# Self attention core: key blocks four heads wide on both row halves, softmax denominators along rows on VectorE, probabilities divided by GpSimd before they are turned

## The reference

```
s[b, h, i, j] = sum_e q[b, h, i, e] * k[b, h, j, e] * 16 ** -0.5     (j > i masked out)
p[b, h, i, :] = exp(s - max_j s) / sum_j exp(s - max_j s)
a[b, h, i, :] = sum_j p[b, h, i, j] * v[b, h, j, :]
x += a @ Wo
```

## Time and profile before

| | us |
|---|---|
| median of the three runs | 3569.16 |
| lowest and highest run | 3563.95 and 3569.59 |
| the profiled execution's own time | 3562.83 |
| its span | 3561.0 |
| TensorE busy in the span | 3273.7 (92%) |
| VectorE, ScalarE, GpSimd busy | 1697.1 (48%), 1383.5 (39%), 550.4 (15%) |

### The profile page before, as it was taken

How to read it: one execution, slowest core, us unless ns; L and a number is a source line. 1 busy time by engine, 2 the same in 40 slices (tenths; PEclk the granted TensorE clock), 3 DMA queues, 4 the chain that set the end, 5 groups by cost and what they waited for, 6 DMA issues and landing times. The chain is left out here.

```text
span 3561.0 us, 57170 instructions
## 1 busy us (share of the span) xinstructions
PE 3273.7 (92%) x22593; PEld 2122.6 (60%) x22597; DVE 1697.1 (48%) x3600; ACT 1383.5 (39%) x2368; POOL 550.4 (15%) x354
## 2 busy tenths in 40 slices
PE   4899999996999789999999889989999999678898
PEld 3567777774445354577777657654577777434444
DVE  5535555543232255566666234345566665455222
ACT  3335665531111132466666122222466666323221
POOL 4322122100216025300000000005200000203000
PEclk8889999997999889999999999999999999878899
DMA  1032221311211112022211110012122221100011
GB/s 29 26 104 55 61 63 47 62 38 52 88 59 56 40 33 67 20 50 51 51 47 36 45 33 28 23 40 67 28 48 44 49 51 32 32 11 21 27 40 35
DMA packets 184554, 158.98 MB, mean 45 GB/s; under 512 B 77780, under 2 KB 155590, under 8 KB 182352
## 3 DMA queue, kind: packets, MB, share of 16 engines
q1 hardware_dynamic: 184288, 155.32, 16.3%
HBM read 115.16 MB, written 18.09 MB: 37 GB/s over the span
## 5 line engine op out<-in xcount | busy, mean ns | idle before, releaser
L1720 ACT ACTIVATE l1x_shared<-l1x_shared,l1x_a_low 128x1500 f32<-128x1500 f32 x112 | 173.1, 1545 | 189.5 <-DVE l1x_shared L1676 189.5
L1720 ACT ACTIVATE l2x_shared<-l2x_shared,l2x_a_low 128x1500 f32<-128x1500 f32 x112 | 173.1, 1546 | 188.7 <-DVE l2x_shared L1676 186.4
L1720 ACT ACTIVATE l0x_shared<-l0x_shared,l0x_a_low 128x1500 f32<-128x1500 f32 x112 | 173.3, 1547 | 187.1 <-DVE l0x_shared L1676 178.0
L1611 PE MATMUL l0x_a_T_ps<-ident,l0x_shared 128*125 128x128 f32 x1344 | 176.1, 281 | 15.5 <-issue 14.7
L1611 PEld LDWEIGHTS l0x_a_T_ps<-ident,l0x_shared 128*125 128x125 f32 x1344 | 155.2, 187 | 39.6 <-issue 38.0
L1611 PE MATMUL l2x_a_T_ps<-ident,l2x_shared 128*125 128x128 f32 x1344 | 176.5, 281 | 0.8 <-ACT l2x_shared L1720 0.8
L1611 PE MATMUL l1x_a_T_ps<-ident,l1x_shared 128*125 128x128 f32 x1344 | 176.5, 281 | 0.8 <-ACT l1x_shared L1720 0.8
L1595 PE MATMUL l1x_a_S_ps<-l1x_kt,l1x_a_q 64*128 64x375 f32 x896 | 172.0, 501 | 1.4 <-DMA l1x_a_q<-l1x_qa 0.8
L1611 PEld LDWEIGHTS l2x_a_T_ps<-ident,l2x_shared 128*125 128x125 f32 x1344 | 155.2, 187 | 29.8 <-issue 28.2
L1611 PEld LDWEIGHTS l1x_a_T_ps<-ident,l1x_shared 128*125 128x125 f32 x1344 | 155.1, 187 | 29.8 <-issue 28.2
L1595 PE MATMUL l0x_a_S_ps<-l0x_kt,l0x_a_q 64*128 64x375 f32 x896 | 172.2, 501 | 0.5 <-DVE l0x_shared L1676 0.5
(11 more groups left out here) (654 smaller groups left out, 6164.9 us busy)
## 6 DMA issues: line engine op xcount, KB each, us to landing
l0f_gu<-in_L_ffn_gu SPq DMA_DIRECT2D x36, 256.0 KB, 2.6
l0x_a_q<-l0x_qa SPq DMA_DIRECT2D x64, 96.0 KB
l1x_a_q<-l1x_qa SPq DMA_DIRECT2D x64, 96.0 KB, 2.3
l2a_w<-in_L_attn_qkv SPq DMA_DIRECT2D x16, 384.0 KB, 3.0
l2x_a_q<-l2x_qa SPq DMA_DIRECT2D x64, 96.0 KB, 2.3
l0x_raw<-in_ctx SPq DMA_DIRECT2D x16, 375.0 KB
kv_rotated<-l0x_v SPq DMA_DIRECT2D x16, 375.0 KB
kt_rotated<-l0x_kt SPq DMA_DIRECT2D x16, 375.0 KB, 4.6
```

The lines of the kernel that those rows point to most:

```text
L1611: last = pe.transpose(T_ps[0:KP, g, kk * 128:(kk + 1) * 128], p[:, n % 2, j % HJ // 3 * 2 + j // HJ, j % 3 * KP:(j % 3 + 1) * KP], m.ident[:])
L1720: act.activation(p[:, n % 2], p[:, n % 2], ACT.Exp, bias=low[:, n % 2, 1:2], scale=-1.0, accum_out=den[:, b % 2, k:k + 1]).then_inc(exp_re ...
```

## The change

It changes `attention_core` and one constant. Key blocks are now four heads wide and cover all 128 partitions: a block of one hf holds both sequences, 128 x (2 x 4 x 64), and partitions 0 to 63 carry heads 0 to 3 of the half, 64 to 127 heads 4 to 7. There are two such blocks for a tile, both made by GpSimd. `scores` uses them by row halves r: each matmul contracts 64 rows and writes 64 x 256, four of them for each hf, and the mask is added in four matmuls of the same 64 x 64 shape. The matmuls with `sum_four` and `spread_four` are gone (both constants stay). VectorE sums the exponentials of a row with a reduction and inverts 128 x 16 sums; GpSimd then multiplies the 128 x 1024 exponentials by the inverses in place, and only then they are turned. `probs` has three buffers in place of two. VectorE no longer makes a key block nor multiplies the output.

```diff
-        kb = st.sb(name + "k_blocks", [128, 2, 2, 2, 8, SP])
-        mask = st.sb(name + "mask", [SP, 8, SP], BF16)
-        sm = st.sb(name + "probs", [128, 2, H, SP])
+        kb = st.sb(name + "k_blocks", [128, 2, 2, 2, 4, SP])
+        mask = st.sb(name + "mask", [128, 4, SP], BF16)
+        sm = st.sb(name + "probs", [128, 3, H, SP])
...
-        inv = st.sb(name + "inverse", [128, SP])
+        den = st.sb(name + "denominators", [128, 2, H])
+        inv = st.sb(name + "inverses", [128, 2, H])
...
-        k_pool = st.sem(name + "k_pool")
-        k_dve = st.sem(name + "k_dve")
+        k_ready = st.sem(name + "k_ready")
...
-        inv_spread = st.sem(name + "inv_spread")
+        summed = st.sem(name + "summed")
+        weighed = st.sem(name + "weighed")
...
-        normed = st.sem(name + "normed")
...
-        def k_block(eng, n, b, hf):
+
+        def k_block(eng, n, hf):
             return eng.tensor_tensor(
-                kb[:, n % 2, b, hf], kt[:, hf, n * 128 + b * SP:n * 128 + (b + 1) * SP].unsqueeze(1).to_broadcast([128, 8, SP]),
-                m.head_mask[:].unsqueeze(2).to_broadcast([128, 8, SP]), ALU.mult)
+                kb[:, n % 2, hf],
+                kt[:, hf, n * 128:(n + 1) * 128].rearrange("p (b k) -> p b k", b=2).unsqueeze(2).to_broadcast([128, 2, 4, SP]),
+                m.four_mask[:].unsqueeze(1).unsqueeze(3).to_broadcast([128, 2, 4, SP]), ALU.mult)
...
-                for n in range(NT):
+                def k_blocks(n):
                     if n > 1:
                         pool.wait_ge(scores_ready, n - 1)
-                    for b, hf in ((0, 0), (1, 0), (0, 1)):
-                        k_block(pool, n, b, hf).then_inc(k_pool, 1)
-                    if n == 0:
-                        pool.memset(vb[:], 0.0).then_inc(zeroed, 1)
+                    for hf in range(2):
+                        k_block(pool, n, hf).then_inc(k_ready, 1)
+
+                k_blocks(0)
+                pool.memset(vb[:], 0.0).then_inc(zeroed, 1)
+                k_blocks(1)
+                for n in range(NT):
+                    pool.wait_ge(inv_ready, n + 1)
+                    pool.tensor_tensor(sm[:, n % 3], sm[:, n % 3], inv[:, n % 2].unsqueeze(2).to_broadcast([128, H, SP]),
+                                       ALU.mult).then_inc(weighed, 1)
+                    if n + 2 < NT:
+                        k_blocks(n + 2)
...
-                    pe.wait_ge(k_pool, 3 * n + 3)
-                    pe.wait_ge(k_dve, n + 1)
+                    pe.wait_ge(k_ready, 2 * n + 2)
...
                     for hf in range(2):
                         for b in range(2):
-                            pe.matmul(S_ps[n % 2][b * SP:(b + 1) * SP, hf, :],
-                                      qt[:, hf, n * 128 + b * SP:n * 128 + (b + 1) * SP],
-                                      kb[:, n % 2, b, hf].rearrange("p h k -> p (h k)"), start=True, stop=False)
+                            for r in range(2):
+                                half = slice(r * 64, (r + 1) * 64)
+                                pe.matmul(S_ps[n % 2][b * SP:(b + 1) * SP, r, hf * 256:(hf + 1) * 256],
+                                          qt[half, hf, n * 128 + b * SP:n * 128 + (b + 1) * SP],
+                                          kb[half, n % 2, hf, b].rearrange("p h k -> p (h k)"),
+                                          start=True, stop=False)
                         for b in range(2):
-                            last = pe.matmul(S_ps[n % 2][b * SP:(b + 1) * SP, hf, :], m.ident_b[0:SP, 0:SP],
-                                             mask[:].rearrange("p h k -> p (h k)"), start=False, stop=True)
+                            for r in range(2):
+                                half = slice(r * 64, (r + 1) * 64)
+                                last = pe.matmul(S_ps[n % 2][b * SP:(b + 1) * SP, r, hf * 256:(hf + 1) * 256],
+                                                 m.ident_b[half, half], mask[half].rearrange("p h k -> p (h k)"),
+                                                 start=False, stop=True)
...
-                    if n > 2:
-                        pe.wait_ge(normed, n - 2)
...
                 def turn(n):
-                    pe.wait_ge(exps_ready, n + 1)
+                    pe.wait_ge(weighed, n + 1)
                     if n > 0:
                         pe.wait_ge(pt_ready, n)
-                    for p in range(8):
-                        last = pe.transpose(T_ps[:, p, :], sm[:, n % 2, 2 * p:2 * p + 2, :].rearrange("q h k -> q (h k)"),
-                                            m.ident[:])
+                    for hf in range(2):
+                        for r in range(2):
+                            for two in range(2):
+                                h = 8 * r + 4 * hf + 2 * two
+                                last = pe.transpose(T_ps[:, 4 * hf + 2 * r + two, :],
+                                                    sm[:, n % 3, h:h + 2, :].rearrange("q h k -> q (h k)"), m.ident[:])
...
-                        pe.wait_ge(inv_ready, n)
-                    for pp in range(4):
-                        for b in range(2):
-                            for hf in range(2):
-                                k = 32 * (2 * b + hf)
-                                pe.matmul(A_ps[k:k + 32, 2, 0:SP], m.sum_four[:, pp, :],
-                                          pt[:, n % 2, hf * 4 + pp, b * SP:(b + 1) * SP], start=(pp == 0), stop=(pp == 3))
...
-                def spread(n):
-
-                    pe.wait_ge(inv_ready, n + 1)
...
-                    for hf in range(2):
-                        for b in range(2):
-                            last = pe.matmul(V_ps[:, 2 + hf, b * SP:(b + 1) * SP], m.spread_four[:, 2 * b + hf, :], inv[:],
-                                             start=True, stop=True)
-                    last.then_inc(inv_spread, 1)
...
-                    if n > 0:
-                        spread(n - 1)
                     values(n)
-                spread(NT - 1)
...
-                def k_last(n):
-                    if n > 1:
-                        dve.wait_ge(scores_ready, n - 1)
-                    k_block(dve, n, 1, 1).then_inc(k_dve, 1)
...
-                    if 1 < n + 1 < NT:
-                        k_last(n + 1)
                     dve.wait_ge(top_ready, n + 1)
+                    if n > 2:
+                        dve.wait_ge(turned, n - 2)
+                    dve.tensor_tensor(sm[:, n % 3], S_ps[n % 2][:].rearrange("q a (h k) -> q (a h) k", k=SP),
+                                      top[:, n % 2].unsqueeze(2).to_broadcast([128, H, SP]), ALU.subtract).then_inc(shifted, 1)
+
+                def invert(n):
+                    dve.wait_ge(exps_ready, n + 1)
+                    dve.tensor_reduce(den[:, n % 2], sm[:, n % 3], AX.X, ALU.add).then_inc(summed, 1)
+                    dve.wait_ge(summed, n + 1)
                     if n > 1:
-                        dve.wait_ge(turned, n - 1)
-                    dve.tensor_tensor(sm[:, n % 2], S_ps[n % 2][:].rearrange("q a (h k) -> q (a h) k", k=SP),
-                                      top[:, n % 2].unsqueeze(2).to_broadcast([128, H, SP]), ALU.subtract).then_inc(shifted, 1)
-
-                def invert(n):
-                    dve.wait_ge(out_ready, n + 1)
-                    if n > 0:
-                        dve.wait_ge(inv_spread, n)
-                    dve.reciprocal(inv[:], A_ps[:, 2, 0:SP]).then_inc(inv_ready, 1)
-
-                def normalise(n):
-                    dve.wait_ge(inv_spread, n + 1)
-                    dve.wait_ge(out_kept, n + 1)
-                    at = m.at[:, :, n * 128:(n + 1) * 128]
-                    dve.tensor_tensor(at, at, V_ps[:, 2:4], ALU.mult).then_inc(normed, 1)
-
-                dve.tensor_copy(mask[:], m.causal[0:SP, :].unsqueeze(1).to_broadcast([SP, 8, SP])).then_inc(mask_ready, 1)
...
-                k_last(0)
-                k_last(1)
+                        dve.wait_ge(weighed, n - 1)
+                    dve.reciprocal(inv[:, n % 2], den[:, n % 2]).then_inc(inv_ready, 1)
+
+                dve.tensor_copy(mask[:], m.causal[:].unsqueeze(1).to_broadcast([128, 4, SP])).then_inc(mask_ready, 1)
                 shift(0)
                 shift(1)
+                invert(0)
                 for n in range(NT):
                     if n + 2 < NT:
                         shift(n + 2)
-                    if n > 0:
-                        normalise(n - 1)
-                    invert(n)
-                normalise(NT - 1)
+                    if n + 1 < NT:
+                        invert(n + 1)
 
...
-                    if n > 1:
-                        act.wait_ge(normed, n - 1)
...
-                    act.wait_ge(inv_ready, n + 1)
-                    act.copy(m.at[:, :, n * 128:(n + 1) * 128], A_ps[:, 0:2]).then_inc(out_kept, 1)
                     if n + 2 < NT:
                         exps(n + 2)
+                    act.wait_ge(out_ready, n + 1)
```

(5 more changed lines are left out.)

10 lines of the change are left out of this document (3 added, 7 removed).

## The result

| | before | after |
|---|---|---|
| median of 4 runs each, same chip | 3567.23 us (3563.95 to 3569.59) | 3623.11 us (3618.05 to 3628.11) |
| ratio, 95% interval | | 1.0178 [1.0163, 1.0192] |
| profiled execution | 3562.8 us, span 3561.0 | 3628.11 us, span 3626.3 |
| three attention stages, sum | 188.7 us | 248.0 us |

The change makes the kernel 1.8% slower: 55.9 us between the medians, 65.3 us between the two profiled executions. The forecast was 3629 us, +62.7; the median lies inside its narrower range, 3615 to 3643.

The account below looks back on a forecast made before the run. No full engine but a serial ring of waits between GpSimd, TensorE and VectorE, 10.55 us a tile, bounds the changed stages; three stages of 83.8 us give +62.7 on 3566.4, so 3629 us, range 3604 to 3655, narrower 3615 to 3643.

Parts of the forecast that it names:

- What comes: a ring: Each tile passes serially through multiplication, next key blocks, scores, shift, sums with inversion and hand-overs: 10.55 us against 6.80.
- Turn ... beside the ring: The turn of n, 1.1 us or 1.9 at low clock, runs while GpSimd makes the key blocks, adding nothing.
- The clock: TensorE, idle over 4 us a tile, runs turn and most scores at its low clock: scores 2.3 us, not 1.4.
- the clock holds: Rival, 15%: TensorE stays at full clock, scores 1.4 us, 9.65 us a tile, 78 us a stage, +45, 3611 us.
- The third buffer ... is worth nothing: The third buffer of probs removes only a wait for the turn outside the serial chain, so it gains nothing.
- Ends of a stage: Start to tile 0's inverses 11.6 us, six tile steps 63.3, last part 8.9: stage 83.8 us.
- The tail: Stage end after tile 6's inverses: multiply, turns, ScalarE copies, values, and 0.45 for a clock below full; 8.9 us.
- The sum: Three attention stages at 83.8 us make 251.4 us, less 188.7 before: +62.7 us.
- time outside the three stages: Sign of being wrong: the kernel's time moves anywhere other than in the three attention stages.
- the ring is open: Rival, 3%: a tile costs only its busiest engine, GpSimd, 4.15 us; stage 45.7 us, total 3515 us.
- The two rules: Skill rules tested against rows: tiling-mode changes drain TensorE, 4 us less in sum; VectorE should multiply, 3 us more.

Follow-up runs that it names:

- a1: Changed kernel with GpSimd making the key blocks of tile n + 2 ahead of the multiplication of n: ratio 1.0174 to the kernel before, stages 247.8 us.
- a4: Changed kernel with four extra unread fp32 matmuls behind the values of each tile but the last two: ratio 1.0119 to the kernel before, stages 230.1 us.
- a5: Changed kernel with two buffers of probs instead of three: ratio 1.0156 to the kernel before, stages 247.0 us.
- a6: Changed kernel with scores and key blocks three tiles ahead, blocks before the multiplication: ratio 0.9875 to the kernel before, stages 149.5 us.
- b1: Kernel before with only the four-wide key blocks on GpSimd and quadrant scores, division as before: ratio 0.9876, repeated 0.9868; stages 143.1 and 142.7 us.
- a2: Changed kernel with VectorE's sums and inversion of tile n + 1 ahead of the shift of n + 2: ratio 0.9955 to the kernel before, stages 167.6 us.
- a3: Changed kernel with key blocks of n + 2 before the multiplication of n, and scores of n + 2 before its turn: ratio 0.9943 to the kernel before.
- a7: a6 with tile 0's sums and inversion moved ahead of tile 1's shift on VectorE: ratio 0.9863 to the kernel before, stages 140.8 us.
- a8: Changed kernel with the multiplication by the inverses on VectorE, GpSimd making key blocks only: ratio 1.0112 to the kernel before, stages 230.1 us.

## Why the prediction was right

- **"What comes: a ring"** held in every link; the maxima are 10.37 us apart in the first stage, 10.55 predicted. The terms: multiplication 1.86 (taken 2.1), key blocks 2.09 with the hand-over to TensorE (2.03 and a part of 0.13), scores until VectorE starts 2.46 (2.3), shift 2.40 (2.48), sums and inversion 1.49 (1.5), the hand-over to GpSimd 0.08. The multiplication and the scores were off in opposite directions.
- **"Turn ... beside the ring"** held only as a tie: at the low clock the turn ends at 122.72, the blocks at 122.69, and the scores start at 122.75. The prediction put the turn at 1.9 and the blocks at 2.03 and didn't see what follows, that taking the blocks away alone frees nothing (a1).
- **"The clock"**: expected low for the turn and most of the scores; it was low for all of the turn, all of the scores and most of the value tokens. The scores were therefore at the upper bound of that term. The rival *the clock holds* put the gain at 18 us (62.7 against 45), and a4, which brings it about, shows 17.9.
- **"The third buffer ... is worth nothing"**: a5 agrees.
- **"Ends of a stage"**: tile 0's inverses came 11.3 us into the stage (11.6). The tail was 10.3 us against 8.9, the term that was worst sized. Its rows:

```profile
162.26 1.97 PE L385 MATMUL l0a_c_T_ps<-ident,l0a_c_probs 128*128 128x128 f32 x8 [3.94 <-POOL l0a_c_probs L329]
164.16 1.98 PE L366 MATMUL l0a_c_V_ps<-l0a_wkv,l0a_hkv 128*64 128x128 f32 x16
...
166.06 1.08 PE L398 MATMUL l0a_c_A_ps<-l0a_c_probs_turned,l0a_c_v_blocks 128*32 128x64 f32 x32
167.07 1.22 PE L385 MATMUL l0a_c_T_ps<-ident,l0a_c_probs 128*128 128x128 f32 x8
...
170.11 0.37 ACT L477 COPY at<-l0a_c_A_ps 128x256 f32<-128x256 f32 x1 [0.77 <-PE l0a_c_A_ps L398]
```

  The prediction's tail went from the turn of tile 6 through ScalarE's copy (1.0) to the values. TensorE's queue has the value tokens of tile 7 in between, 1.9 us at the low clock, and the copy lies beside them. That is 0.9 us, and a turn of 1.9 and values of 1.0 at the low clock, for 1.2 and 0.7, are another 1.0, for which only 0.45 had been set aside. Six shorter turns of the ring (-1.05) and the shorter start (-0.3) hid it: 83.83 for the first stage, 83.8 predicted. That match is in part luck.
- **The sum**: +59.3 us in the stages against +62.7; the second and third stages were 82.3 and 81.8 us long, with turns of the ring of 10.25 and 10.21 us, where the prediction had taken 10.55 for all three. The profiled execution grew by 65.3, so some 6 us lie elsewhere: 12 more between the first and the second stage, 4 fewer ahead of the first and 2 fewer behind the second. The prediction had named time outside the three stages as a sign of being wrong. The scores of layer 0's cross attention, which lie between the first two stages, run over 521 us in the profile after and 513 before, and over 525 to 535 in the profiles of a1, a4, a6 and b1, which are slower and faster kernels alike. So that stretch, whose code the change doesn't touch, is not longer where the kernel is slower; what moves it stays open.
- **The rival that ends on the other side** (the ring is open, 3515 us): it didn't happen, but a2, a3, a6 and a7 make it happen by order alone, a2 and a3 in part (5.2 and 5.8 us a tile). It put a stage at 45.7 us with 4.2 a tile; a7 has 46.4, 46.7 and 47.7, and a6 4.4 a tile.

The two rules. The mask part starts 0.90 us behind the key part in the timeline at the low clock, for 0.86 us of columns (eight records of 256, four at a time, each 0.43 at the low clock, as 512 columns take at the upper one), so a gap of 0.04 stands where there were 0.19, and the next key part starts 0.22 us behind the mask, for 0.21 of columns, where the gap was 0.13; the Trainium skill (TensorEngine Tiling (Array Packing), Key Properties) has a change of tiling mode drain the array, and by that rule the gap should go with the change of shape. The trace agrees, though the size of the matmuls changed together with their shape. It is worth 0.12 us a ring (scores 2.46, halved from before 2.46 and 0.12 for VectorE's start: 2.58), less than the 0.2 that the prediction worked out from it. On the multiplication, GpSimd took 1.90 us and VectorE 1.23 for the same operation, 65% and not the half that the Trainium skill (GPSIMD Engine Reference, Engine selection) gives. Its advice holds here: followed in a8, it makes the stages 17.9 us shorter, some 4 of them by the clock, and the prediction had weighed it at 3 us, because it compared two prices for GpSimd's product and not the two engines.

## What to carry to other kernels

When a change makes one engine wait for a result of another, write down what is queued behind the wait, who waits for that, and go on until the first engine comes up again: if it does, the time of a tile is the sum round that ring, and busy shares say nothing. Cut the ring by the order of calls before making any link cheaper: here one swap was worth 80 us, a faster engine for the multiplication (with some help of the clock) or a kept clock 18 each, and the removal of a single link nothing, since another of the same length lay beside it. Time the parts of a change apart; a part that gains 1.2% alone was buried under one that loses 4.1%.

## What was not expected of the hardware

- GpSimd multiplies 128 x 1024 with one repeated operand in 1.90 us, under both bounds that were taken from its other products (2.03 and 2.25).
- Four quadrants of TensorE work side by side: scores and mask take 1.25 us at full clock (b1) where they took 2.69, less than half, since the gaps between key part and mask went as well.
- Matmuls of which nobody reads the result pay: 3.70 us of them a tile lift the clock of the first stage from 0.68 to 0.92 and shorten the three stages by 17.9 us.
- In every turn of the ring TensorE started at the low level behind its hole and had the upper one back only at the values, its last work of the tile (0.50 until 126, 0.90 in 126 to 128), so that of its work there only the values and the end of the value tokens ran at the upper one. In the seven turns of each stage that waited so, the eight transposes took 1.97 us, where they take 1.09 at the upper level.
